# Softmax weights of a banded attention layer: transposed by DMA as fp16 halves instead of by TensorE

## What is computed

```python
Q, K, V = (heads of) xn @ Wq + bq, xn @ Wk + bk, xn @ Wv + bv        # 16 heads of 64
scores = einsum('bhid,bhjd->bhij', Q, K)                             # 1024 x 1024
band = abs(j - i) <= 64
attn = softmax(where(band, scores, 0.0), axis=-1)                    # zero, not -inf, outside the band
out = (attn @ V) merged over heads @ Wo + bo
s = xn @ Win + bin_                                                  # 64 columns
g = sum_h relu(s[..., None] * W1 + b1) * W2 + b2                     # 16 hidden units each
x + out + (g @ Wout + bout)
```

## Time and profile before

| | us |
|---|---|
| median of 3 runs | 2233.77 (2233.75 to 2234.09) |
| profiled execution, its own time | 2233.51 |
| its span in the trace | 2231.8 |
| TensorE busy | 2154.3 |
| DVE busy | 1832.5 |
| ACT busy | 1514.3 |
| POOL busy | 917.0 |

### The profile page before, as it was taken

How to read it: one execution, slowest core, us unless ns; L and a number is a source line. 1 busy time by engine, 2 the same in 40 slices (tenths; PEclk the granted TensorE clock), 3 DMA queues, 4 the chain that set the end, 5 groups by cost and what they waited for, 6 DMA issues and landing times.

```text
span 2231.8 us, 45652 instructions
## 1 busy us (share of the span) xinstructions
PE 2154.3 (97%) x16263; PEld 1310.0 (59%) x16263; DVE 1832.5 (82%) x5062; ACT 1514.3 (68%) x4217; POOL 917.0 (41%) x1313
## 2 busy tenths in 40 slices
PE   6879899999999999999999999999999999999998
PEld 4445565656655666565665666656565666665664
DVE  4667787888788888888888888798878888888877
ACT  4666676777667667676667666676767767667665
POOL 3756644533253342533244343353334334253323
PEclk8889999999999999999999999999999999999999
DMA  3121211301112110221112111031111211021111
GB/s 102 58 85 39 77 35 33 114 29 34 34 48 88 37 39 24 73 76 30 30 30 85 59 39 29 30 109 34 30 38 48 86 39 38 22 76 30 34 34 48
DMA packets 69760, 112.94 MB, mean 51 GB/s; under 512 B 6664, under 2 KB 18976, under 8 KB 69536
## 3 DMA queue, kind: packets, MB, share of 16 engines
q1 hardware_dynamic: 69488, 110.02, 15.7%
q10 hardware_dynamic: 48, 0.01, 0.0%
HBM read 84.84 MB, written 25.17 MB: 49 GB/s over the span
## 4 chain that ended last, share of the span: by engine, by line
PE 82%; DVE 10%; POOL 2%; ACT 2%; DMA 1%; issue 1%; SPq 1%; DVEq 0%; ACTq 0%; POOLq 0%
PE ps L1183 38%; PE ps L1198 13%; PE ps L1236 9%; PE ps L1169 8%; PE ps L1249 8%; PE ps L1226 3%; DVE acc L880 2%; DVE pT_lo L927 2%; DVE probs L852 2%; DMA w_raw<-in_L_attn_Wk 1%; PE ps L1109 1%; PE ps L1220 1%; PE ps L1208 1%; DVE xn L898 1%; DVE v_mean L932 1%
## 5 line engine op out<-in xcount | busy, mean ns | idle before, releaser
L1183 PE MATMUL ps<-xT_hi,w_split 128*128 128x512 f16 x3072 | 986.2, 382 | 17.4 <-POOL w_split L336 15.8
L371 POOL TENSOR_SCALAR probs<-probs,inv_l,neg_e 128x256 f32<-128x256 f32 x1024 | 568.6, 572 | 815.7 <-DVE neg_e L871 815.7
L495 ACT ACTIVATE probs<-probs,neg_max 128x256 f32<-128x256 f32 x1024 | 506.2, 497 | 154.7 <-DVE neg_max L859 154.4
L1183 PE MATMUL ps<-xT_lo,w_split 128*128 128x512 f16 x1536 | 586.8, 382 | 0.0
L1183 PEld LDWEIGHTS ps<-xT_hi,w_split 128*128 128x128 f16 x3072 | 302.7, 99 | 364.0 <-issue 24.3
L852 DVE CUSTOM_DVE_ANT_0 probs<-ps,mask,unit_s 128x256 f32<-128x256 f32 x1024 | 433.7, 480 | 59.6 <-PE ps L1169 56.1
L880 DVE SCALAR_TENSOR_TENSOR acc<-ps,unit_o,acc 128x512 f32<-128x512 f32 x512 | 370.9, 743 | 86.8 <-PE ps L1198 85.7
L550 ACT ACTIVATE pT_hi<-ps 128x512 f16<-128x512 f32 x512 | 276.2, 597 | 189.9 <-PE ps L1249 166.6
L927 DVE TENSOR_TENSOR pT_lo<-ps,pT_hi 128x512 f16<-128x512 f32 x512 | 322.2, 682 | 16.3 <-ACT pT_hi L550 16.1
L1198 PE MATMUL ps<-wo_split,oT_hi 128*128 128x512 f16 x1024 | 309.6, 384 | 11.3 <-DVE top_used L758 4.1
L378 POOL TENSOR_TENSOR oT_lo<-o_sum,oT_hi 128x512 f16<-128x512 f32 x128 | 148.6, 1161 | 410.7 <-ACT o_sum L563 410.7
(11 more groups left out here) (123 smaller groups left out, 2925.3 us busy)
## 6 DMA issues: line engine op xcount, KB each, us to landing
w_split<-w_kept SPq DMA_DIRECT2D x168, 256.0 KB, 2.6
acc<-in_L_attn_x SPq DMA_DIRECT2D x14, 1024.0 KB, 6.8
out_x<-acc SPq DMA_DIRECT2D x14, 1024.0 KB, 4.6
wo_split<-wo_kept SPq DMA_DIRECT2D x56, 256.0 KB, 2.7
w_kept<-w_split SPq DMA_DIRECT2D x24, 256.0 KB, 4.7
acc<-in_L_attn_x SPq DMA_DIRECT2D x4, 512.0 KB, 5.3
w_raw<-in_L_attn_Wv SPq DMA_DIRECT2D x8, 256.0 KB, 5.1
w_raw<-in_L_attn_Wq SPq DMA_DIRECT2D x8, 256.0 KB, 5.5
```

The lines of the kernel that those rows point to most:

```text
L371: pool.tensor_scalar(probs[:, h, t], probs[:, h, t], inv_l[:, c:c + 1], neg_e[:, c:c + 1], ALU.mult, ALU.add).then_inc(normed, 1)
L495: act.activation(probs[:, h, t], probs[:, h, t], ACT.Exp, bias=neg_max[:, c:c + 1], accum_out=row_sum[:, c:c + 1])
L1183: last = pe.matmul(dst[:], w[wp][:, i, c], xT[xp][:, c, half * LINE:half * LINE + LINE], start=(c == 0 and a == 0), stop=(c == KC - 1 and ...
```

## The change

- The weights are no longer transposed by TensorE. After `normalise_weights`, ACT copies `probs` to fp16 (`weights_high(half, h)`, one instruction of 128x1024 for each head and half) and POOL makes the low half (`weights_low(half, h)`, 128x1024). SP then issues a transposing DMA for each half, head and part (eight a step, 128x1024 fp16 each) to `pT[half][h][part]`.
- `weigh_values`, `weighted_sums` and `output_low` work on pair o = n - 2, one step later, ahead of `project_out` of the same pair in the same step. `v` and `v_back` get two buffers for it.
- `mask_scores` waits until the low half of the pair before has read `probs`.
- `w_raw` and `wo_raw` have two buffers and are loaded two pairs ahead. The low halves of the weights are made by DVE in one instruction (`split_low`, `split_output_low`), not by POOL in two.
- The order on every engine and the bank tables are new. Network work is spread in fours: hidden units 4(k-1) to 4(k-1)+3 in pairs 1 to 4, statistics four each in pairs 3 and 4.
- To make room in SBUF, `bias_2` and `wout_raw` share memory with `o_sum`, and `squares` has one buffer.

The core of the diff:

```diff
-        w_raw = sb("w_raw", [P, 3, KC, P])
+        w_raw = sb("w_raw", [P, 2, 3, KC, P])
...
-        v = sb("v", [P, T, 2, 2, D], F16)
+        v = sb("v", [P, 2, T, 2, 2, D], F16)
         probs = sb("probs", [P, 2, T, WIN])
-        pT = [[sb(f"pT{i}_{part}", [P, 2 * LINE], F16) for part in ("hi", "lo")] for i in range(2)]
+        p_split = [sb(f"p_{part}", [P, 2, T, WIN], F16) for part in ("hi", "lo")]
+        pT = [[[sb(f"pT{half}{h}_{part}", [P, 2 * T // 2, P], F16) for part in ("hi", "lo")] for h in range(2)] for half in range(2)]
...
-        SCORE_BANK = ((2, 4), (3, 1), (7, 2), (0, 4))
-        V_BANK, VT_BANK = (5, 2), (4, 6)
-        QK_BANK = (6, 5, 7, 7)
-        OUT_BANK = (5, 1, 1, 3, 7, 1, 6, 0)
-        PT_BANK = ((1, 6), (0, 4), (0, 2), (6, 3))
-        PV_BANK = (5, 3)
-        XT_BANK = (7, 2, 2, 4, 7, 5, 3, 2)
-        FIRST_XT_BANK = (7, 2, 0, 4)
-        FFN_IN_BANK = (7, 3)
-        FFN_OUT_BANK = ((0, 7), (1, 7), (2, 0), (7, 0))
+        SCORE_BANK = ((0, 1), (2, 3), (0, 1), (4, 5))
+        V_BANK, VT_BANK = (3, 1), (6, 7)
+        QK_BANK = (7, 2, 2, 3)
+        OUT_BANK = (7, 0, 4, 5, 7, 0, 4, 5)
+        PV_BANK = (6, 5)
+        XT_BANK = (6, 0, 4, 1, 7, 0, 1, 6)
+        FIRST_XT_BANK = (4, 5, 0, 2)
+        FFN_IN_BANK = (6, 1)
+        FFN_OUT_BANK = ((6, 3), (0, 1), (6, 4), (6, 3))
...
+            def transpose_weights(j, half, h, part):
+                u = 2 * half + h
+                if 2 * j - 1 + half > 0:
+                    sp.wait_ge(pv_done, 2 * j - 1 + half)
+                sp.wait_ge((p_hi, p_lo)[part], 4 * j + u + 1)
+                sp.dma_start_transpose(pT[half][h][part][:],
+                                       p_split[part][:, h, 4 * half:4 * half + 4].rearrange("p t w -> p (t w)")) \
+                    .then_inc(pT_in[half], 16)
...
+                if 2 <= n <= PAIRS + 1:
+                    keep_output(n - 1, n - 2)
+                elif out_proj:
+                    load_output_kept(n - 1, (k - 2) % PAIRS)
+                if split and k > 0:
+                    load_output_raw(k)
+                if k == 2 and b > 0:
                     store(b - 1, 1)
-                if k == 3 and not last:
-                    load_x(b + 1, 1)
-                if loads_next:
-                    load_kept(n, V_, next_pair)
-                if k == 1 and proj:
+                if k in (2, 3) and not last:
+                    load_x(b + 1, k - 2)
+                if attend:
+                    transpose_weights(j, 0, 0, hi)
+                    transpose_weights(j, 0, 1, hi)
+                    transpose_weights(j, 0, 0, lo)
+                    transpose_weights(j, 0, 1, lo)
+                if k == 1 and b > 0 and proj:
                     store(b - 1, 0)
-                if k == 2 and not last:
-                    load_x(b + 1, 0)
-                if loads_next:
-                    load_kept(n, Q_, next_pair)
-                    load_kept(n, K_, next_pair)
-                if n == PAIRS:
-                    keep_output(n, PAIRS - 1)
-                elif attend:
-                    load_output_kept(n, (k - 1) % PAIRS)
+                if proj:
+                    next_weights(V_)
+                    next_weights(Q_)
+                if attend:
+                    transpose_weights(j, 1, 0, hi)
+                    transpose_weights(j, 1, 1, hi)
+                if proj:
+                    next_weights(K_)
+                if n == PAIRS - 1:
+                    first_kept(V_)
+                    first_kept(Q_)
+                if attend:
+                    transpose_weights(j, 1, 0, lo)
+                    transpose_weights(j, 1, 1, lo)
+                if n == PAIRS - 1:
+                    first_kept(K_)
...
+                def weights_low(half, h):
+                    tiles = slice(4 * half, 4 * half + 4)
+                    pool.wait_ge(p_hi, 4 * j + 2 * half + h + 1)
+                    pool.tensor_tensor(p_split[lo][:, h, tiles], probs[:, h, tiles], p_split[hi][:, h, tiles],
+                                       ALU.subtract).then_inc(p_lo, 1)
...
+                    output_low(0)
                 if attend:
                     normalise_weights(0)
-                if 0 < n <= PAIRS:
+                if n <= PAIRS:
                     inverse_root(tops_of_step(n), top_ready, scaled_in(n), root_ready)
-                if k == 1 and proj and b > 0:
-                    add_biases(2)
-                if attend:
-                    normalise_weights(1)
...
-                if split_next:
-                    split_low(n + 1, V_)
-                    split_low(n + 1, Q_)
+                if attend:
+                    weights_low(0, 0)
+                    weights_low(0, 1)
+                if out_proj:
+                    output_low(1)
...
-                if attend:
-                    output_low(0)
+                if k == 1 and proj and b > 0:
+                    add_biases(2)
...
+                if attend:
+                    normalise_weights(1)
+                    weights_low(1, 0)
+                    weights_low(1, 1)
...
-                def weights_high(u, c):
-                    if c == 0 and 2 * j + u // 2 > 0:
-                        act.wait_ge(pv_done, 2 * j + u // 2)
-                    act.wait_ge(p_T, 8 * j + 2 * u + c + 1)
-                    act.activation(pT[u % 2][hi][:, c * LINE:c * LINE + LINE], ps[PT_BANK[u][c]][:], ACT.Copy) \
-                        .then_inc(pT_hi, 1)
+                def weights_high(half, h):
+                    tiles = slice(4 * half, 4 * half + 4)
+                    if j > 0:
+                        act.wait_ge(pT_in[half], 64 * j)
+                    act.wait_ge(normed, 16 * j + 8 * half + 4 * h + 4)
+                    act.activation(p_split[hi][:, h, tiles], probs[:, h, tiles], ACT.Copy).then_inc(p_hi, 1)
...
+                if out_proj:
+                    weighted_sums(0)
+                if attend:
+                    exps(0)
+                    exps(1)
                 if proj:
                     qk_high(0)
...
+                if attend:
+                    exps(2)
+                if proj:
+                    qk_high(1)
+                if attend:
+                    weights_high(0, 0)
...
+                if attend:
+                    exps(3)
...
+                if proj:
+                    value_lines(0)
+                if attend:
+                    weights_high(0, 1)
+                if out_proj:
+                    weighted_sums(1)
+                hidden_high(0)
...
+                if proj:
+                    value_lines(1)
...
+                hidden_high(1)
+                if split_next:
+                    split_high(n + 1, V_)
...
                 if attend:
                     weights_high(1, 0)
+                if proj:
+                    qk_high(2)
+                if split_next:
+                    split_high(n + 1, Q_)
+                hidden_high(2)
...
+                if attend:
+                    weights_high(1, 1)
...
                 if proj:
                     qk_high(3)
+                if split_next:
+                    split_high(n + 1, K_)
                 if proj:
                     values_high(0)
                     values_high(1)
...
+                hidden_high(3)
                 if attend and n <= PAIRS:
+                    split_output_high(j)
...
+            def split_low(n, i):
+                dve.wait_ge(w_hi[i], n + 1)
+                dve.scalar_tensor_tensor(w[lo][:, i], w_raw[:, n % 2, i], w_scale[:, n, i:i + 1], w[hi][:, i],
+                                         ALU.mult, ALU.subtract).then_inc(w_lo[i], 1)
+
+            def split_output_low(pair):
+                dve.wait_ge(wo_hi, pair + 1)
+                dve.scalar_tensor_tensor(wo[lo][:], wo_raw[:, pair % 2], w_scale[:, pair + 2, 3:4], wo[hi][:],
+                                         ALU.mult, ALU.subtract).then_inc(wo_lo, 1)
...
+                    if j > 0 and tp % 2 == 0:
+                        dve.wait_ge(p_lo, 4 * j - 2 + tp)
...
+                if attend:
+                    mask_scores(0)
+                    mask_scores(1)
+                    mask_scores(2)
+                    denominators(0)
+                    mask_scores(3)
+                if proj:
+                    qk_low(0)
...
+                if proj:
+                    qk_low(1)
+                if n <= PAIRS:
+                    read_tops(tops_of_step(n), TOP_BANK, top_sum, scaled_in(n), top_ready)
...
+                row_statistics(0)
...
+                if attend:
+                    denominators(1)
+                if n <= PAIRS:
+                    step_scales(n)
...
+                if out_proj:
+                    add_output(0)
+                    add_output(1)
...
+                hidden_unit(0)
+                row_statistics(1)
...
                 if out_proj:
+                    add_output(2)
```

(91 more changed lines are left out.)

811 lines of the change are left out of this document (253 added, 558 removed).

## The result

The changed kernel takes 2254.1 us at the median of four executions (2249.4 to 2260.6), the kernel before 2233.9 in the same session: 1.0092 times as long, 95% interval 1.0065 to 1.0119, so 0.9% slower. The forecast was 2052 us, range 1968 to 2160. The profiled execution took 2249.37 us, its span is 2247.6.

A forecast was written before the change was run, and what follows sets the result against it. TensorE, 97% busy, was taken as the bound, with the new loop next. Head 420, body 6 x 246 = 1476 and tail 154 gave a span of 2050, so 2052 us, 8.1% faster; range 1968 to 2160.

The forecast's parts named there:

- the prediction's own sign: Steady image: under 240 us or over 252 us would show the forecast of 246 us wrong.
- rival B: Port shared by POOL and DVE decides: image 256 us, head 440, tail 158, total 2136 us; chance 0.16.
- The bound: TensorE limits the body; removing 32 transposes frees 3.65 us a step, 31.73 to 28.08 us.
- The loop: Masks, exponentials, POOL, ACT copies and q/k splits: 28.7 us against TensorE's 28.1; 9.5 us an image with network work.
- The port: POOL/DVE port collisions: at worst two waits a step of 1.2 us, half in slack, giving 256 us an image.
- one short collision: Pairs 1 to 4 of the loop: 3.8 us of hidden units and row statistics, rounded to 4.0 with it.
- The copies and GpSimd's load: ACT copies 1.3 us each, POOL subtractions 2.32 us each; POOL busy near 70%.
- The transposes: SP's DMA queue: eight transfers a step, 1 to 2.5 us of queue each, 10 us of cover, cost nothing.
- Rival C: Transposing queue is the bound: 256-byte rows, about 5 us each, 43 us a step, some 2830 us; chance 0.12.
- Head and tail: Start and end of the span: head 477.6 to 420 us, tail 160.3 to 154 us.
- half of 45 us: First image: 29 us without TensorE work plus 16 us of lost clock, of which 22 us come back.
- Rival D: Freed 3.65 us a step return as stalls over 3 us, then the clock falls; within 0.2% of before; chance 0.02.

The follow-up runs named there:

- e2: Changed kernel without GpSimd's low halves of the weights; transfers and masks use the high halves instead: 2097.95 us in a single run.
- e4b: Kernel before with 8 instead of 32 TensorE transposes of weights a step, copies reading one block four times: 2174.66 us in a single run.
- e11: Changed kernel with each low half written by four one-input GpSimd instructions of 128x256 (probs times zero) instead of the two-input subtraction: 2220.6 us.
- e3: Changed kernel with ScalarE's qk_high(2) and qk_high(3) moved ahead of the copies (1,0) and (1,1): 2228.1 us, 0.9969 of the kernel before.
- small kernels: Separate kernels without attention: one VectorE probe begun inside GpSimd chains, with phase and company varied; a small probe took 2.14 us against 2.08 us subtractions.
- e12: Changed kernel with half 0's low halves behind normalise_weights(1), their transposes behind those of half 1's high halves: 2373.0 us, 1.0622 of the kernel before.
- e1: Changed kernel with all transposing DMAs replaced by plain copies of the same 256 KB: 2249.3 us, 1.0075 of the kernel before.
- e13: e12 plus e3's ScalarE order and the centring of the values on ScalarE: 2483.1 us, 1.1122 of the kernel before.
- m1: First of the small kernels: VectorE probes of several forms against GpSimd chains of low halves or normalisings; the PSUM probe never waited (0.69 us).

## Why the prediction was wrong

**Where the miss lies.** Cut as the prediction cuts the span, at the first q projection of the fifth pair in the second and the eighth image (463.2 and 2083.2 us), the changed kernel has a head of 463.2, a body of 1620.0 and a tail of 164.4 us, against 420, 1476 and 154. Of 198 us 144 are in the body, 24 an image. Without the low halves (e2) the three are 428.4, 1510.5 and 156.8. By the prediction's own sign, an image over 252 us, this is its rival B, and more than B's 256 us an image.

**The bound.** That TensorE bounds the kernel before was right, but not enough to go by. The prediction took 3.65 us a step as the freed time and asked only what the new order's loop adds. It never asked how far the other engines stood behind TensorE in the old one; e4b puts that at 0.8 us a step, in the old order. Even without low halves the new order returns 13.9 of 29.2 us an image (e2).

**The loop.** Right in its place: e11's chain and the changed kernel's own run through it piece by piece, and e3 takes 2 us out of pair 5. Its length was put at 28.7 us (its pieces add up to 28.6), and a bare step takes 31.0 to 31.2. The changed kernel's chain shows where: three pieces of it are collisions between VectorE and GpSimd, and cost 2.0 of the 2.4 us.

```profile
735.17 1.03 DVE neg_max L858
...
750.48 1.61 POOL oT_lo L393
...
758.61 1.40 DVE xn L901
```

Undisturbed, the negation takes 0.17 us, the output's low half 1.16, and a hidden unit 0.66 of the chain. The masks also start 3.1 us into the step and not 2.8.

**The port.** This is the step that failed, and with it goes most of the miss: the low halves cost 156 of the 202 us, and by the estimate from e11 nearly all of that is the port. The forecast's sum has nothing for it but one short collision. Rival B priced it at two waits a step of 1.2 us on average, halved by slack, 10 us an image. The mechanism was right and the term mis-sized: the low halves cost 18 us an image and 25 in the first. By the table 15.3 of an image's 17.9 us are in pairs 7, 1 and 2, where the waits run over the whole row of GpSimd instructions and not over one: 5.03 us in the centring of pair 7, 5.58 and 3.14 in the hidden unit of pairs 1 and 2, in the first image 5.2 in `row_l`. The earlier trace rows was misread. The prediction says that `v_mean` once took 2305 ns, as the wait for one instruction. It took 2157 to 2305 ns seven times, once in each image from the second on, and over two bias adds of 1.3 us: that wait already spanned a boundary. The Trainium skill (SBUF — State Buffer, "Who interferes with whom") says that the shared ports are locked for a whole instruction and the loser blocks. The small kernels agree (2.14 us by a 2.08 us instruction). In the large kernel the 8.74 us in e12, over four instructions, go beyond it, and so did the 2305 ns of the kernel before, which the prediction took as agreeing; the measurement decides.

**The copies and GpSimd's load.** A copy takes 1.05 us for 1.3, a low half 2.16 for 2.32, and GpSimd is busy for 62% where 70 were expected. All near, and of no use, since the price was not GpSimd's busy time.

**The transposes.** Right: free, with 3.1 and 3.3 us to landing against 10 us of cover. The share of 16 DMA engines went from 15.7% to 49.3%, more than the byte count asks (e1 moves the same bytes at 32.2%). By these shares of the spans a transfer keeps the queue for about 1.5 us, an estimate, inside the 1 to 2.5 us taken, and a plain one for 0.7. Rival C had the pieces right, 256 bytes each (1024 to a transfer in the trace), but not what they cost. Where the cover goes they do cost (e12). The 1309 ns of the Trainium skill for a 128x128 block (VectorE: DVE Perf Modes, "The three transpose paths") are not a price that adds up here: eight blocks land in 3.1 us.

**Head and tail.** The first scores come 10.9 us earlier, but the first image gained only 7.8 us where I counted on its 3.65 a step and half of 45 us besides. Its granted clock is 0.89, not over 0.94. Five `row_l` waits of 5.2 us stand there, and a wait that the prediction missed (total us, times, longest):

```profile
ACT w_split L471 <- DMA w_kept<-w_split: 41.5, 16, 4.4
```

`split_high` waits until the kept halves are stored, and that store now stands on SP's queue behind the transposes. The new order moved the reloads past the new transfers, not the stores. What this wait costs no run shows: e2 has 43.3 us of it, and a first image of 243.2 us. The tail was to shrink by 6 us and grew by 4, by the prediction's cut. From the last scores to the end it is 11.7 us; e2's stretch is 42.1, so the low halves are 2.5 of that, and the rest I can't name. The granted clock there is 0.80, with 25 us of TensorE work in 44.7.

**The clock.** The mean granted clock fell from 0.985 to 0.953. By steps of one image it is 0.91 in pair 7, where stretches at 0.50 (1.2 GHz) follow an idle of 4.7 us, 0.95 to 0.96 in pairs 0 to 3, and 1.00 again from pair 4. Rival D named this and had 0.02. It is no whole explanation: the clock loses 4 to 9% in five of eight steps, and e2, with the same order and no long waits, has 0.98 in the mean.

**Chances.** Slower had 0.13, of which 0.12 was the queue. The sign turned on the port, which I let end at 2136 us.

## What to carry to other kernels

Before counting freed time on the busiest engine as gained, take a part of that work out and measure: here an engine that was 97% busy gave back a third. When GpSimd gets long two-operand instructions, list every VectorE instruction with two SBUF operands that can fall beside them, and those with one too (the centring and the negation waited, the `v_new` of one column didn't). Price the wait at the whole row of GpSimd instructions, and keep it off the loop. And remedies on one queue don't add up (45 us for 82 here): moving a stalled instruction pays only up to the next consumer behind it.

## What the hardware showed

VectorE's wait for GpSimd is booked as busy time (187 us here), so a mean that is far over a group's shortest is the sign to look for. It ends at the next boundary in small kernels and often not in the large one (5.58 us in the changed kernel, 8.74 in e12, 11.6 in e13). GpSimd's one-input form is slower to fp16 than to fp32 in this kernel (857 ns for 586 at 128x256, both in e11). Normalisings let VectorE in after the one that runs: a wide VectorE instruction makes eight of them 4.80 us long instead of 4.30 (m1). A transposing DMA of 256 KB lands in 3.1 us, in 1024 packets of 256 bytes; a plain one (2.3 us) has 128 of 2048 bytes.
